# Attention's order at both ends, and Mamba's rows, inputs and late z, in a two-layer hybrid tower on one core

## The reference, cut to what matters

```
h = attention16(x)                       # 16 heads of 16, width 256, S = 512
h = concat(cls, h)                       # T = 513 tokens
h = h + diag_ssm(layernorm(h))           # gated linear recurrence of 256 states
h = h + conv_ffn(layernorm(h))           # BitNet feed-forward, 1024 wide, conv of 3 taps, silu
h = h + mamba(layernorm(h))              # below
h = h + gated_ffn(layernorm(h))          # BitNet silu(gate) * up, 1024 wide

mamba(x): xv, z = split(x @ W_in.T)      # 512 channels each
          xv = silu(causal_conv4(xv)); dt = softplus(x[:, :64] @ W_dt.T + b)
          Bm = x @ W_B.T; Cm = x @ W_C.T # 16 states each
          for each state n: h_n = exp(dt*A_n) * h_n + dt*xv * Bm[:, n];  y += h_n * Cm[:, n]
          return (y * silu(z)) @ W_out.T
```

## Time and profile before

| | |
|---|---|
| median of 3 runs | 2689.73 us (2687.26 to 2691.68) |
| the profiled execution's own time | 2690.58 us |
| its span, first to last instruction | 2688.8 us |
| mean granted TensorE clock | 0.928 |
| busy: PE, DVE, ACT, POOL | 2102.5, 2080.8, 1281.0, 1211.9 us |

### The profile page before, as it was taken

How to read it: one execution, slowest core, us unless ns; L and a number is a source line. 1 busy time by engine, 2 the same in 40 slices (tenths; PEclk the granted TensorE clock), 3 DMA queues, 4 the chain that set the end, 5 groups by cost and what they waited for, 6 DMA issues and landing times.

```text
span 2688.8 us, 24367 instructions
## 1 busy us (share of the span) xinstructions
PE 2102.5 (78%) x8636; PEld 1142.2 (42%) x8636; DVE 2080.8 (77%) x2361; ACT 1281.0 (48%) x1810; POOL 1211.9 (45%) x567
## 2 busy tenths in 40 slices
PE   2898877777799886777779997677877998867786
PEld 0226652235423664224542475322453246632254
DVE  6864869986885578997788467899687847789967
ACT  1564366553165436653327544566323744455632
POOL 1110259991211116997222110899521212289932
PEclk9999988998999998999899999899989999989898
DMA  5200000000120000000022000000003100000000
GB/s 177 86 13 0 1 0 0 0 0 1 68 84 1 1 1 0 0 0 0 1 86 65 1 1 0 0 0 0 0 1 114 37 1 1 0 0 0 0 0 16
DMA packets 41072, 51.26 MB, mean 19 GB/s; under 512 B 9072, under 2 KB 32368, under 8 KB 40944
## 3 DMA queue, kind: packets, MB, share of 16 engines
q1 hardware_dynamic: 40944, 49.62, 5.8%
HBM read 26.25 MB, written 10.49 MB: 14 GB/s over the span
## 4 chain that ended last, share of the span: by engine, by line
PE 48%; DVE 23%; POOL 14%; issue 8%; ACT 6%; DMA 1%; SPq 0%; POOLq 0%; DVEq 0%; ACTq 0%
PE psum L667 15%; PE psum L931 12%; POOL big L1761 10%; PE psum L796 5%; POOL big L1750 4%; PE psum L770 3%; PE psum L784 3%; DVE mid L1297 3%; ACT big L1009 3%; DVE mid L1565 3%; PE psum L729 2%; ACT mid L1009 2%; PE psum L803 2%; PE psum L686 2%; DVE mid L1230 2%
## 5 line engine op out<-in xcount | busy, mean ns | idle before, releaser
L931 PE MATMUL psum<-big,ident 128*128 128x512 f32 x992 | 528.4, 682 | 202.1 <-POOL big L1761 201.8
L1631 DVE TENSOR_TENSOR_SCAN big<-psum,b,big 128x512 f32<-128x512 f32 x512 | 614.2, 1262 | 0.0
L1009 ACT ACTIVATE big<-psum 128x1024 f32<-128x1024 f32 (+2 forms) x592 | 450.4, 777 | 302.3 <-PE psum L784 160.2
L1761 POOL TENSOR_TENSOR big<-big 128x2048 f32<-128x2048 f32 x124 | 560.0, 4517 | 22.3 <-DVE big L1631 22.3
L1009 ACT ACTIVATE psum<-mid,aneg 128x512 f32<-128x512 f32 x512 | 353.9, 692 | 265.0 <-DVE big L1631 265.0
L931 PEld LDWEIGHTS psum<-big,ident 128*128 128x128 f32 x992 | 203.9, 216 | 485.1 <-POOL big L1761 264.3
L1399 DVE TENSOR_REDUCE negmax<-psum 128x1 f32<-128x512 f32 x512 | 318.2, 679 | 26.7 <-PE psum L770 25.5
L1750 POOL TENSOR_TENSOR big<-mid,big 128x512 f32<-128x512 f32 (+1 forms) x128 | 222.2, 1736 | 19.9 <-ACT big L1009 19.9
L770 PE MATMUL psum<-mid 96*128 96x512 bf16 x512 | 189.2, 383 | 24.8 <-DVE negmax L1399 23.7
L784 PE MATMUL psum<-mid 98*128 98x512 bf16 x512 | 186.0, 382 | 21.0 <-ACT big L1009 10.8
L1009 ACT ACTIVATE mid<-mid 128x513 f32<-128x513 f32 (+2 forms) x112 | 97.9, 899 | 201.6 <-DVE mid L1283 201.4
(11 more groups left out here) (185 smaller groups left out, 3434.6 us busy)
## 6 DMA issues: line engine op xcount, KB each, us to landing
mid<-mid SPq DMA_DIRECT2D x192, 64.0 KB, 2.6
mid<-scratch SPq DMA_DIRECT2D x192, 64.0 KB, 2.2
scratch<-big SPq DMA_DIRECT2D x4, 1536.0 KB, 6.1
out<-hres SPq DMA_DIRECT2D x8, 513.0 KB, 5.3
big<-in_x SPq DMA_DIRECT2D x8, 512.0 KB, 4.5
big<-in_w SPq DMA_DIRECT2D x2, 1024.0 KB, 6.3
big<-in_wg SPq DMA_DIRECT2D x1, 1024.0 KB, 10.0
big<-in_wu SPq DMA_DIRECT2D x1, 1024.0 KB, 11.9
```

Of the source, the lines that this page charges most:

```text
L931: mm = nc.tensor.matmul(y_psum[:, c], ident[:, :], st(1, k)[:, c], start=(n == 0), stop=(n == NS - 1))
L1009: return nc.scalar.activation(o, a, func, **kw)
L1631: V.tensor_tensor_scan(st(0, k)[:, c], a_psum(DT * k + c), st(0, k)[:, c], b0[:, p, n, c:c + 1], ALU.mult, ALU.add).then_inc(scanned, 1)
L1761: G.tensor_tensor(st(1, k), st(0, k), c_row(k).unsqueeze(1).broadcast_to([P, DT, S]), ALU.mult).then_inc(hc_ready, 1)
```

## The change

**Attention.** LAG_ST goes from 6 to 8; steps 8 to 15 take five shifted tiles instead of four, so that the backlog is gone at step 16. The values of groups 0 and 1 start at step 12. Sequence 1's q and k products move into steps 0 to 3, and v into steps 4 to 7, with DVE's `split_qk(1, s - 1)` a step later. POOL's two memsets of padding wait until DVE has split sequence 0 (`qk_rest` of 12), and PE waits for them only at the first shifted tile. Sequence 1's normalised groups get buffers of their own (`normed`), and the dummy products at the end become 4 before the last group only (they were 10 before each of the last two).

**Feed-forward.** q = 1: the maximum is taken in two halves of four tiles. q = 3: ACT takes the absolute value of each product tile, and DVE keeps a running maximum, a tensor_tensor per tile.

**Mamba.** B and C are no longer split: DVE copies the 32 rows to SBUF in f32, SP stores them in DRAM, and loads each row spread over the partitions, B and C, into four buffers each. PE spreads only B, in f32 out of 32 rows, for DVE. ACT's two copies per step go. The inputs come in a new order. Sequence 1's z is made inside the scan (`late_z` after steps 3, 6, 9 and 12), ACT copies it out of PSUM at the third decay of the same step, and takes its silu after the scan. Sequence 1's dt*xv moves from POOL to DVE.

```diff
-WARM_O = 10
+WARM_O = 4
+MAMBA_FILLS = [(f"d{c}", 0) for c in range(DT)] + [("x0", 0), ("x1", 0)] + [(f"d{c}", 1) for c in range(DT)] \
+    + [("x2", 0), ("x3", 0), ("bc", 0), ("bc", 1), ("x0", 1), ("x1", 1)] + [(f"z{c}", 0) for c in range(DT)] \
+    + [("x2", 1), ("x3", 1)]
+Z_STEPS = (3, 6, 9, 12)
+ROWS = 4
-LAG_ST, LAG_PV = 6, 10
+LAG_ST, LAG_PV = 8, 10
...
# SP
+                for k in range(PAIR * NS):
+                    p, n = divmod(k, NS)
...
+                    if k >= ROWS:
+                        sp.wait_ge(b_pool, k - ROWS + 1)
+                    sp.dma_start(b_row(k), bc_dram[p, n:n + 1, 1:T].broadcast_to([P, S])).then_inc(b_in[k % ROWS], 16)
+                    if k >= ROWS:
+                        sp.wait_ge(hc_ready, k - ROWS + 1)
+                    sp.dma_start(c_row(k), bc_dram[p, NS + n:NS + n + 1, 1:T].broadcast_to([P, S])).then_inc(
+                        c_in[k % ROWS], 16)
...
# PE, the head of attention
-                pe.wait_ge(x_in[1], i * 16 + 16)
-                heads_product(QK_ORDER[0], 1)
-                heads_product(QK_ORDER[1], 1)
                 pe.wait_ge(qk_rest, 4)
-                pe.wait_ge(pads, 2)
...
# PE, the scan
                 def spread_b(k):
                     if k:
-                        pe.wait_ge(b_copied, k)
-                    spread_row(k, k % NS, b_psum).then_inc(b_spread, 1)
+                        pe.wait_ge(b_used, k)
+                    r = k % NS
+                    nc.tensor.matmul(b_psum, ident[0:2 * NS, r:r + 1].broadcast_to([2 * NS, P]),
+                                     bc_rows(k // NS)[:, 1:T], start=True, stop=True).then_inc(b_spread, 1)
+                def late_z(c):
+                    if c:
+                        pe.wait_ge(z_raw, c)
...
+                    for k in range(KT):
+                        mm = nc.tensor.matmul(z_psum, wz[:, k, c * P:(c + 1) * P], big_un(1)[:, k, 1:T],
+                                              start=(k == 0), stop=(k == KT - 1))
+                    mm.then_inc(z_full, 1)
                 spread_b(0)
-                spread_c(0)
-                spread_b(1)
                 for k in range(PAIR * NS):
-                    if k + 2 < PAIR * NS:
-                        spread_b(k + 2)
                     if k + 1 < PAIR * NS:
-                        spread_c(k + 1)
+                        spread_b(k + 1)
                     if k:
                         add_y(k - 1)
+                    if k in Z_STEPS:
+                        late_z(Z_STEPS.index(k))
# ACT, in the loop over the four decays of step k
-                            if c == 1:
-                                if k >= 2:
-                                    act.wait_ge(hc_ready, k - 1)
-                                act.wait_ge(c_spread, k + 1)
-                                run(c_row(k), c_psum, ACT.Copy).then_inc(c_copied, 1)
-                                if k + 1 < PAIR * NS:
-                                    copy_b(k + 1)
+                            if c == 2 and k in Z_STEPS:
+                                zc = Z_STEPS.index(k)
+                                act.wait_ge(z_full, zc + 1)
+                                run(mid4(1, 1)[:, zc, 1:T], z_psum, ACT.Copy).then_inc(z_raw, 1)
# DVE
+                def half_max_of(p, n):
+                    V.tensor_reduce(mid1(p, (6, 7)[n]), big8(p, 1)[:, 4 * n:4 * n + 4].rearrange("p c t -> p t c"), AX_X,
+                                    ALU.max, apply_absolute_value=True).then_inc(half_max, 1)
+                    if n:
+                        dve.wait_ge(half_max, 2 * p + 2)
+                        V.tensor_tensor(mid1(p, 6), mid1(p, 6), mid1(p, 7), ALU.max).then_inc(absmax_part, 1)
+                def running_max(p, c):
+                    dve.wait_ge(prod_abs, HT * p + c + 1)
+                    if c > 1:
+                        dve.wait_ge(prod_max, (HT - 1) * p + c - 1)
+                    V.tensor_tensor(mid1(p, 6), mid1(p, 6), mid1(p, 4 + c % 2), ALU.max).then_inc(prod_max, 1)
...
+                V.tensor_tensor(mid4(1, 3), mid4(1, 2), mid4(1, 0), ALU.mult).then_inc(dtx_ready, 1)
# POOL
+                pool.wait_ge(qk_rest, 12)
                 G.memset(k_stack[ROWS_MAX:KROWS, :, :], 1.0).then_inc(pads, 1)
```

More of the change, by code:

```diff
@@ L130, in plan_fills @@
     ln(3)
[L131 to L134, removed]
+    while len(order) % 4:
+        order.append(None)
+    order.extend(MAMBA_FILLS)
     while len(order) % 4 != 2:
@@ L1162, in _, with silu @@
-                nc.scalar.preload_act_table(ACT.Silu)
-                for c in range(DT):
-                    first_tap(1, c)
-                    act.wait_ge(m_tap, 3 * c + 3)
-                    run(mid4(0, 0)[:, c], mid4(0, 0)[:, c], ACT.Silu).then_inc(m_silu, 1)
-                for c in range(DT):
+                def silu(p, c):
+                    act.wait_ge(m_tap, 3 * (DT * p + c) + 3)
+                    run(mid4(p, 0)[:, c], mid4(p, 0)[:, c], ACT.Silu).then_inc(m_silu, 1)
+                for c in range(DT):
+                    step_input(0, c)
@@ new lines, in _, with silu_z @@
+                absolute(0)
+                first_tap(0, 0)
+                first_tap(0, 1)
+                exponential(0)
+                for c in range(DT):
+                    step_input(1, c)
+                logarithm(0)
+                first_tap(0, 2)
+                absolute(1)
+                first_tap(0, 3)
+                exponential(1)
+                first_tap(1, 0)
+                logarithm(1)
+                nc.scalar.preload_act_table(ACT.Silu)
+                def silu_z(c):
@@ L1168, in _ @@
                     wait_full(act, f"z{c}", 0)
                     run(mid4(0, 1)[:, c], slot(f"z{c}", 0), ACT.Silu).then_inc(z_silu, 1)
-                    act.wait_ge(m_tap, 3 * (DT + c) + 3)
-                    run(mid4(1, 0)[:, c], mid4(1, 0)[:, c], ACT.Silu).then_inc(m_silu, 1)
-                for c in range(DT):
-                    wait_full(act, f"z{c}", 1)
-                    run(mid4(1, 1)[:, c], slot(f"z{c}", 1), ACT.Silu).then_inc(z_silu, 1)
+                first_tap(1, 1)
+                silu(0, 0)
@@ new lines, in _ @@
+                silu(0, 1)
+                silu_z(0)
+                silu(0, 2)
+                silu_z(1)
+                silu(0, 3)
+                silu_z(2)
+                silu_z(3)
+                silu(1, 0)
+                first_tap(1, 2)
+                silu(1, 1)
+                first_tap(1, 3)
+                act.wait_ge(first_full, 1)
+                run(mid4(1, 1)[:, :, 0], z_psum[:, 2 * PAIR * NS:2 * PAIR * NS + DT], ACT.Silu).then_inc(z_first, 1)
+                run(first[:, :, :].rearrange("p b r -> p (b r)"), z_psum[:, 0:2 * PAIR * NS], ACT.Copy).then_inc(
+                    first_copied, 1)
@@ L1175, in _ @@
+                silu(1, 2)
+                silu(1, 3)
                 load_ln_exp()
-                act.wait_ge(first_full, 1)
-                run(first[:, :, :].rearrange("p b r -> p (b r)"), c_psum[:, 0:PAIR * 32], ACT.Copy).then_inc(
-                    first_copied, 1)
                 act.wait_ge(dt_ready, PAIR)
-                act.wait_ge(bc_split, 6 * PAIR)
-                def copy_b(k):
-                    if k >= 2:
-                        act.wait_ge(b_pool, k - 1)
-                    act.wait_ge(b_used, k + 1)
-                    run(b_row(k), b_psum, ACT.Copy).then_inc(b_copied, 1)
@@ L1568, in _, with round_up, taps @@
-                for p in range(PAIR):
+                def round_up(p):
+                    dve.wait_ge(sp_act, 3 * p + 2)
+                    affine2(big4(p, 1), mid4(p, 3), 1.0, 1.0, ALU.add, ALU.subtract).then_inc(sp_round, 1)
+                def taps(p, c):
+                    k = DT * p + c
+                    dve.wait_ge(m_tap0, k + 1)
+                    xp, acc = slot(f"x{c}", p), mid4(p, 0)[:, c]
+                    for n in range(1, 4):
+                        if n > 1:
+                            dve.wait_ge(m_tap, 3 * k + n - 1)
+                        V.scalar_tensor_tensor(out=acc[:, n:T], in0=xp[:, 0:T - n], scalar=col("mw", 4 * c + 3 - n),
+                                               in1=acc[:, n:T], op0=ALU.mult, op1=ALU.add).then_inc(m_tap, 1)
@@ L1840 @@
     scratch = nc.dram_tensor("scratch", (3, 4, P, S), BF16, kind="Internal").ap()
+    bc_dram = nc.dram_tensor("bc_rows", (PAIR, 2 * NS, T), F32, kind="Internal").ap()
     out = nc.dram_tensor("out_0", (B, KT, P, T), F32, kind="ExternalOutput").ap()
-    build(nc, x, w, scratch, out)
+    build(nc, x, w, scratch, bc_dram, out)
     r = _run(nc, [arrays], core_ids=[0])
```

326 lines of the change are left out of this document (176 added, 150 removed).

## The result

The changed kernel takes 3016.2 us (median of 4 runs, 3013.1 to 3019.0) against 2690.3; the ratio is 1.121, interval 1.119 to 1.123. I had forecast 2935, with 2835 to 3010: the direction was right, the size too small by 81 us, and the time lies above the range.

The account below looks back on a forecast made before the run. In the scan DVE and POOL were taken as full. Scan 49 + 13 + 19 = 81 us a turn slower, less 19.3 of gains, is 61.7; four turns, 247, on 2690.6 give 2937; forecast 2935, range 2835 to 3010.

Parts of the forecast that it names:

- The loop: Scan: DVE's spread of m+3 also waits for addition of m; two steps 15.6 us (two-tile loop 15.1), +49 us a turn.
- The clock: PE in the scan: half the additions start at the lower clock, 1.7 us more each, 13 us a turn slower.
- The late z: Scan steps 3, 6, 9, 12: ACT waits for z before the fourth decay, 12.5 us against 7.8; 19 a turn slower.
- The gains: Mamba's inputs, attention's head and end, and both maxima: 7 + 5 + 2.8 + 1.5 + 3 = 19.3 us a turn faster.
- Attention: Head of attention 5 us a turn faster (bounds 2 and 9), end of attention 2.8 (bounds 2 and 3.5).
- Mamba's inputs: Before the scan: first recurrence at 391 instead of 397.88, a gain of 7 us a turn (bounds 2 and 11).
- Maxima: Feed-forward: q = 1 gains 1.5 us a turn (bounds 0 and 3), q = 3 gains 3 (bounds 7 and -3).
- DVE and POOL standing in each other's way: q = 3's running maxima: two-SBUF-input DVE instructions and POOL exclude each other; if all met one, total 24 us higher.
- A: PE between C product and DVE's next spread: the addition does not come in DVE's way, gains stay, 2613 us; chance 0.06.
- B: Scan: the loop is there, but the clock stays full and ACT's wait for z is hidden, 2810 us; chance 0.09.
- C: PE in the scan: whole additions at the lower level, 7.4 us, B product 1.85; total 3160 us; chance 0.05.
- D: Row loads in the scan: two of 256 KB a step come late; at 5 us each, 3200 us; chance 0.03.

Follow-up runs that it names:

- both order experiments: PE's B row of step k+1 instead of k+2 made in iteration k of the kernel before: 2951.0 us; the opposite edit in the changed kernel: 2744.8 us.
- dummies_both: Changed kernel with dummy PE products ahead of the addition in each step, 14 in odd and 8 in even ones: 2928.7 us, ratio 1.090.
- z_copy_later: Changed kernel, its order kept, with only ACT's copy of z out of PSUM two steps later: 2930.5 us, ratio 1.089.
- attention_only: Kernel before with only the attention part of the change: 2670.0 us, ratio 0.993.
- the two versions above: Changed kernel, B-row order put back, z copied two steps later, POOL's first spread after DVE's first-token instructions: 2630.3 us; plus dummies before second B row: 2624.5 us.
- before_order_new: Kernel before with one edit, PE makes the B row of step k+1 in iteration k instead of k+2's: 2951.0 us, ratio 1.098.
- order_back: Changed kernel with the B row of step k+2 made in iteration k again, all else as changed: 2744.8 us, ratio 1.021.
- dummies: Changed kernel with 14 dummy PE products between B row and addition in every second step: 3007.9 us, ratio 1.119.

## Why the prediction was right in its mechanism and too small in its size

**The loop.** Right. "DVE's spread of m+3 waits for the addition of m as well" is what the waits, the timelines and both order experiments show. At full clock 15.6 us for two steps was said, and dummies_both ran at 15.6 on the mean. That it fits so well is partly luck: the B product, of which no row was there, was taken at 0.93 and measured 1.05 to 1.12, while POOL's product, taken at 4.51, took 3.81 in two steps of four.

**The clock: the step that failed.** "I take half, bounds none and all. Each adds 1.7 to its two-step loop, 0.85 a step: 30 x 0.5 x 0.85 = 13 us a turn." This term was mis-sized. Some half of the additions are slow, that was right: in the first turn 17 of the 30 that the trace shows whole, at 5.29 to 6.77 us, 5.74 on the mean (of the kernel before I had counted about 12 of 31; its trace has 10). But they don't fall evenly. The additions come in pairs, one close behind the other, except where a late z breaks the pair up. The 17 longer ones stand behind 5.1 to 7.2 us of idle PE, but for one behind 3.25; the 13 of 3.70 stand behind 1.92 at most. The longest is this:

```profile
495.85 6.77 PE L995 MATMUL psum<-big,ident 128*128 128x512 f32 x8 [6.12 <-POOL big L1874]
```

So one of the two interleaved loops has the slow addition each time: the one with two tiles, but for two places among the z steps. By the prediction's own rule the longer rules, so both steps pay for it, and the term had to be reckoned as all slow, each at 2.0 over 3.70 and not 1.7. Term by term from the rows, that loop is the 15.1 of the prediction, plus 2.0 for the addition and 0.15 for the B product, less 0.35 since POOL's product is 4.16 on the mean: 16.9, measured 17.1. I had written of a loop at full clock and then averaged over it. What the runs showed in place of the 13: dummies_both took 22 us a turn away, half of it in the loop and half in the z steps. In z_copy_later, with no z in the way, DVE's spreads wait for 74.5 us a turn, where the prediction's loop and clock together came to 62. How the 22 divide exactly is open, since the two costs share additions. My estimate of the idle time, 3.1 us a step, was about right as a mean; it came as 5 to 6 us once per two steps.

**The late z.** The mechanism was right, the size a little low: 12.5 us a step were said, and from the end of the recurrences at 415.02 to that at 429.14 it was 14.1, since the addition in it took 5.93 instead of 3.70, while POOL's product took 3.81 instead of 4.51. Removing it gave 21 a turn for my 19. Taken together the scan cost 92.9 a turn, 81 predicted: 48 of the 81 us of error.

**The gains.** 19.3 a turn were said, 11.4 came: 32 us of error. *Attention:* 5 a turn alone, of 7.8. The casts of the head take 0.43 us in the changed kernel and none is held up any more, and the first scores did come 2.6 earlier in attention_only, as said, but the 5 us of the head were an estimate on a fuller DVE list, and of those no more than half arrived; which step of the head kept the rest I did not separate. *Mamba's inputs:* 2.8 of 7 on the mean. I had the first recurrence at 391, it came at 392.9, in a turn that was at its norm 1.7 us ahead. Rows show time that the prediction had not put in: 3 us of L1668 and 3 us of L1736 stopped beside POOL, and B products of 2.07. What each was worth is known for the last two alone, 2.8 and 1 us a turn by the two versions above. *Maxima:* q = 3 gave 3.2 in the changed kernel's trace, as said; q = 1 nothing that shows, of 1.5; alone they gave 2.0 by the medians.

**DVE and POOL standing in each other's way.** The prediction weighed it where it did not decide. In the second block of the first turn the running maxima that its timeline shows singly took 0.68 to 1.06 us, and the gain of q = 3 was the 3 us without it. But before the scan, with both inputs in SBUF, L1668 took 5.36 against 2.29, and L1736 1.19 and 2.09 against 0.22 once POOL was made to wait. I applied the rule of the Trainium skill (SBUF — State Buffer, "Who interferes with whom") to one edit and not to the one next to it, where the new order put POOL's additions beside DVE's dt, and POOL's first spreads beside small DVE products. These rows fit the rule.

**The rivals.** A (the addition not in DVE's way) fell with before_order_new. B (z hidden, full clock) fell: ACT waited for z for 33.8 us in the first turn. C (whole additions at the lower level) did not come: the longest of the changed kernel is 6.77, not 7.4, and the mean of the 17 is 5.74. D (late rows) fell with order_back; the loads of the changed kernel landed in 3.8 us (median), three steps ahead of use:

```profile
big<-bc_rows SPq DMA_DIRECT2D x256, 256.0 KB, 3.8
```

The range's upper end had "all slow, z at 25 and small gains" at 3051, which I called unlikely and cut to 3010. These were no independent mishaps: a slow addition in each loop also lengthens each z step.

## What to carry to other kernels

When a product is moved by one place in an in-order list, write down what now stands ahead of it and who waits for it; here three lines cost 260 us. If such a loop has an idle gap of 5 to 7 us ahead of a PE burst, as here, reckon every burst on the path as slow (5.74 us for 3.70 here), and don't average over two loops of which the longer rules. A copy out of PSUM belongs where its product has long been done: two steps later was worth 86 to 104 us.

## What the runs showed of the hardware that I had not expected

POOL's product of 128x2048 by a row spread over four tiles takes 4.51 or 3.81 us by where the row's buffer lies: with the four buffers at the end of the tile 4.51, with the other four 3.81, and after a shift of the first four by 10 words (40 bytes, which gives both groups the same offset within 64 bytes) 3.81 for all 31 of a turn. In the kernel before, the C rows lie elsewhere in the tile, but at the offset within 64 bytes of the slow group, and all 31 took 4.51. Only one shift was tried, so that it is the offset within 64 bytes, and not some other effect of the address, is not shown.

The idle time just before a burst doesn't settle alone at which level it runs: in the kernel before, bursts behind 2.48 us and 2.49 us of it took 3.70 and 5.40 us, while a burst behind 2.85 us in dummies took 5.40 and one behind 1.01 us and dummies in dummies_both 3.70.
